# A CIN and tower kernel on one core: the tower run in two groups of batch rows, the context share summed in PSUM, and five ACT banks for each tile of the last chunk

## The chip, the cores and the metric

The kernel runs on one core of a Trainium2 chip. The metric is the device time of one execution, in microseconds (us). Before the change it is 917.98 us, the median of 3 runs (917.52 to 918.87).

## The reference, cut to what matters

For each of 512 batch rows, 32 embedding rows of 32 numbers are gathered (`e`). Two layers of outer products follow, then a small tower of three dense layers.

```python
z = einsum('bhd,bmd->bhmd', e, prev)         # prev = e in layer 0, cur in layer 1
cur = relu(einsum('bpd,pn->bnd', z, W[0]))   # n = 128; layer 1 has 32 * 128 products p
z = sum(concatenate([cur0, cur1], axis=1), axis=-1)   # pooled over d: 256 numbers a row
h = concatenate([z, dense_ctx], axis=1)      # 256 + 16 = 272 numbers a row
h = maximum(h @ W_top1 + b_top1, 0.0)        # 512
h = maximum(h @ W_top2 + b_top2, 0.0)        # 256
y = h @ W_top3                               # 1
```

## The kernel before

**Tiles and banks.** The 512 rows are four blocks of 128 (`BT = 4`). A chunk is one block and four values of d (`DC = 4`), so there are 32 chunks and 128 tiles (`TILES`), a tile being 128 rows and one d. Layer 1 of a tile is 8 banks of 128x512: a bank is four fields h of 128 outputs each, made by three passes of TensorE (`three_passes`: high by high, high by low, low by high, all 512 columns). What TensorE writes for a field must still be scaled by the embedding number of that row and field, and the 32 fields be added up. The banks of a tile are shared between two engines. The first `DQ` of them (4, 3, 4, 3 for the four tiles of a chunk) go through the PSUM tile `yd` (3 buffers) to VectorE, which scales and adds in one instruction a field (`add_bank`). The other 4 or 5 (`AQ`) go through `ya` (2 buffers) to ScalarE, which only scales them into `scaled` (`scale_bank`).

**What is done with ScalarE's part.** GpSimd starts a DMA that adds one half of the tile's first four banks to the other (`halve`), then adds what is left (`sum_up`: L310, L314 only for a fifth bank, L318) into `part`. VectorE starts its chains from `part`, so that it waits for it in its first bank. At a tile's end `join_chains` adds the two chains, and `add_to_sum1` adds the tile into the pooled sum of its block, `pooled1_b`.

**Order.** Every engine runs an order written out by hand, each instruction with the semaphores that it waits for. TensorE goes through slots, one for each tile: in a slot it makes in turn an A bank (for ScalarE) of this tile and a D bank (for VectorE) of the tile three before (`LAG = 3`). After the slot of tile 127 there are no A banks, and D banks of tiles 125, 126 and 127 alone are left. While a chunk runs, layer 0 of the next one is made between its slots.

**The tower** comes after the last tile, for all 512 rows at once. TensorE transposes the pooled sums (L742), ScalarE copies them to SBUF (L495), and TensorE multiplies four pieces of `W_top1` by `pooled0` (L746) and by `pooled1` (L749). VectorE adds `ctx_share` (L642), which is the context's part of layer 1 with the bias, computed at the start of the program (L655 on TensorE, L394 on ScalarE). ScalarE applies the relu (L498), TensorE makes layer 2 (L754), ScalarE its bias and relu (L501), TensorE layer 3 (L760), ScalarE the copy of y (L504), and a DMA from SP's queue writes it. All matmuls of the tower have plain float32 operands; a matmul of them has two records in the trace. Those of the banks have one for each pass.

## Time and profile before

| | |
|---|---|
| device time, median of 3 runs | 917.98 us |
| the profiled execution's own time | 913.96 us |
| its span in the trace | 911.6 us |
| busy TensorE (PE) | 837.5 us, 92% |
| busy VectorE (DVE) | 763.2 us, 84% |
| busy ScalarE (ACT) | 764.8 us, 84% |
| busy GpSimd (POOL) | 661.3 us, 73% |

The span runs from the first to the last instruction or transfer. The profiled execution took 2.36 us more than its span, and 4.02 us less than the median of the three unprofiled runs. Busy time of PE is that of its matmul records, which overlap where they are pipelined, so the start of one to the start of the next is the better measure of what a matmul costs. PEld is TensorE's load of the stationary operand.

### The profile page before, as it was taken

The numbers are of one execution on the slowest core, as the hardware profiler recorded it, in microseconds if no ns is written. First come the engines' busy times: TensorE is split into PE (matmuls) and PEld (weight loads), VectorE is DVE, ScalarE is ACT, GpSimd is POOL, SyncE is SP. The second block draws the span as 40 slices with busy tenths as digits, with TensorE's granted clock in tenths as the row PEclk, the third lists the DMA queues.
The fourth block names the chain that finished last, engine by engine and source line by source line (L and its number), as shares of the span: only waits on it lengthen the run. The fifth ranks groups of instructions, "written<-read, shape, count | busy, mean of one in ns | idle before, by whom it ended". The sixth has DMA issues, their size and how long they took to land.

```text
span 911.6 us, 14382 instructions
## 1 busy us (share of the span) xinstructions
PE 837.5 (92%) x3572; PEld 670.4 (74%) x3572; DVE 763.2 (84%) x2400; ACT 764.8 (84%) x2568; POOL 661.3 (73%) x630
## 2 busy tenths in 40 slices
PE   0317999999999999999999999999999999999988
PEld 0114788887888888887888888878888888888753
DVE  0214799998999999998999999988999999999891
ACT  0315999999999999999999999999999999999842
POOL 6773788887878888887888788865776666667550
PEclk9999999999999999999999999999999999999998
DMA  9145767667766667677676776677666776764430
GB/s 269 17 108 159 164 152 163 145 159 182 165 155 164 144 154 166 154 156 171 158 163 156 159 167 155 145 161 170 152 153 152 165 162 151 157 155 91 84 70 0
DMA packets 57717, 133.83 MB, mean 147 GB/s; under 512 B 8785, under 2 KB 22321, under 8 KB 57538
## 3 DMA queue, kind: packets, MB, share of 16 engines
q0 software_dynamic: 22528, 69.22, 42.1%
q1 hardware_dynamic: 32178, 59.94, 20.2%
q10 hardware_dynamic: 2928, 3.76, 1.4%
q8 instruction: 28, 0.46, 0.2%
q14 instruction: 55, 0.45, 0.1%
HBM read 62.64 MB, written 5.24 MB: 74 GB/s over the span
## 4 chain that ended last, share of the span: by engine, by line
PE 85%; ACT 5%; POOL 4%; DVE 2%; issue 2%; DMA 2%; SPq 0%; DVEq 0%
PE ya L659 14%; PE ya L660 14%; PE ya L661 14%; PE yd L659 10%; PE yd L661 10%; PE yd L660 10%; POOL emb L287 4%; ACT scaled L444 3%; PE acc L659 3%; PE acc L661 3%; PE acc L660 3%; DVE acc L579 1%; DMA x<-xt_scratch 1%; PE acc L682 1%; PE ya L754 1%
## 5 line engine op out<-in xcount | busy, mean ns | idle before, releaser
L444 ACT ACTIVATE scaled<-ya,emb 128x128 f32<-128x128 f32 x2304 | 661.9, 386 | 56.0 <-PE ya L661 49.7
L579 DVE SCALAR_TENSOR_TENSOR acc<-yd,emb,acc 128x128 f32<-128x128 f32 x1408 | 397.0, 341 | 8.1 <-PE yd L661 7.5
L310 POOL TENSOR_TENSOR quarter<-scaled 128x512 f32<-128x512 f32 x128 | 195.8, 1530 | 62.2 <-DMA scaled<-scaled 46.2
L659 PE MATMUL ya<-w_hi,prev_hi 128*128 128x512 f32 x576 | 227.7, 395 | 6.5 <-ACT scaled L444 4.8
L660 PE MATMUL ya<-w_lo,prev_hi 128*128 128x512 f32 x576 | 225.3, 391 | 0.0
L661 PE MATMUL ya<-w_hi,prev_lo 128*128 128x512 f32 x576 | 225.1, 391 | 0.0
L303 POOL DMA_DIRECT2D scaled<-scaled x128 | 117.8, 920 | 104.7 <-ACT scaled L444 94.3
L659 PE MATMUL yd<-w_hi,prev_hi 128*128 128x512 f32 x448 | 175.2, 391 | 2.1 <-DVE pooled_b L598 1.8
L661 PE MATMUL yd<-w_hi,prev_lo 128*128 128x512 f32 x448 | 174.4, 389 | 0.0
L660 PE MATMUL yd<-w_lo,prev_hi 128*128 128x512 f32 x448 | 174.3, 389 | 0.0
L287 POOL DMA_INDIRECT emb<-in_tbl,idx x128 | 134.6, 1052 | 30.7 <-issue 27.2
L659 PEld LDWEIGHTS ya<-w_hi,prev_hi 128*128 128x128 f32 x576 | 108.6, 189 | 36.0 <-ACT scaled L444 11.2
L661 PEld LDWEIGHTS ya<-w_hi,prev_lo 128*128 128x128 f32 x576 | 108.7, 189 | 23.1
L660 PEld LDWEIGHTS ya<-w_lo,prev_hi 128*128 128x128 f32 x576 | 108.8, 189 | 21.5
L531 DVE TENSOR_TENSOR prod<-xb,xm_ps 128x512 f32<-128x512 f32 x128 | 87.7, 685 | 31.1 <-DMA xb<-xt_scratch 27.6
L579 DVE SCALAR_TENSOR_TENSOR acc<-yd,emb,part 128x128 f32<-128x128 f32 x256 | 77.7, 345 | 37.3 <-PE yd L661 32.5
L318 POOL TENSOR_TENSOR part<-quarter 128x256 f32<-128x256 f32 x128 | 100.4, 784 | 10.0
L659 PEld LDWEIGHTS yd<-w_hi,prev_hi 128*128 128x128 f32 x448 | 84.1, 188 | 22.8 <-DVE pooled_b L598 2.9
L661 PEld LDWEIGHTS yd<-w_hi,prev_lo 128*128 128x128 f32 x448 | 84.1, 188 | 17.6
L660 PEld LDWEIGHTS yd<-w_lo,prev_hi 128*128 128x128 f32 x448 | 84.1, 188 | 17.4
L536 DVE TENSOR_TENSOR lo<-prod,hi 128x512 fp32r<-128x512 f32 x128 | 87.2, 681 | 11.5 <-ACT hi L424 11.5
L314 POOL TENSOR_TENSOR quarter<-quarter,scaled 128x512 f32<-128x512 f32 x64 | 82.8, 1294 | 5.0
(69 smaller groups left out, 711.2 us busy)
## 6 DMA issues: line engine op xcount, KB each, us to landing
scaled<-scaled POOLq DMA_DIRECT2D x128, 512.0 KB, 6.7
xb<-xt_scratch SPq DMA_DIRECT2D x64, 512.0 KB, 5.4
x<-xt_scratch SPq DMA_DIRECT2D x64, 192.0 KB
xm<-xt_scratch SPq DMA_DIRECT2D x32, 256.0 KB, 3.0
emb<-in_tbl,idx POOLq DMA_INDIRECT x128, 3.9
scaled<-in_L_rec_filter SPq DMA_DIRECT2D x8, 256.0 KB, 6.3
xt_scratch<-xt_stage SPq DMA_DIRECT2D x7, 256.0 KB, 3.3
xt_scratch<-xt_stage SPq DMA_DIRECT2D x9, 128.0 KB, 3.3
```

The source lines that it names most:

```text
L287: pool.indirect_dma_start(emb[:, bt, D * f:D * (f + 1)], None, tables[f], bass.IndirectOffsetOnAxis(ap=idx[:, bt, f:f + 1], axis=0)).then_ ...
L303: pool.dma_start(piece[:, 0:2 * C], piece[:, 2 * C:4 * C], accum_op=ALU.add).then_inc(halved[tile % PR], 16)
L310: pool.tensor_tensor(four, piece[:, 0:C], piece[:, C:2 * C], ALU.add).then_inc(quartered, 1)
L314: pool.tensor_tensor(four, four, piece[:, 4 * C:5 * C], ALU.add).then_inc(quartered, 1)
L318: pool.tensor_tensor(part[:, tile % PR].rearrange("p i n -> p (i n)"), four[:, 0:2 * N], four[:, 2 * N:4 * N], ALU.add).then_inc(part_read ...
L444: op = act.activation(scaled[:, tile % PR, C * j + N * i:C * j + N * (i + 1)], ya[:, n % RA, N * i:N * (i + 1)], ACT.Copy, scale=scale_of( ...
L531: dve.tensor_tensor(prod[:], xb[:, k, :], xm_ps[:], ALU.mult).then_inc(product_ready, 1)
L536: dve.tensor_tensor(lo[:, n % 2, :], prod[:], hi[:, n % 2, :].bitcast(F32), ALU.subtract).then_inc(lo_ready, 1)
L579: dve.scalar_tensor_tensor(after, y_part, scale_of(tile, HB * j + i), before, ALU.mult, ALU.add).then_inc(chained, 1)
L659: pe.matmul(dst, v_hi, m_hi, start=start, stop=False)
L660: pe.matmul(dst, v_hi, m_lo, start=False, stop=False)
L661: return pe.matmul(dst, v_lo, m_hi, start=False, stop=stop)
```

## The change

**Banks.** In the last chunk every tile has 3 D banks and 5 A banks (`DQ_LAST`), where tiles 124 and 126 had 4 and 4. The functions `dq(tile)` and `aq(tile)` take the place of the tuples.

**The last tile's part.** GpSimd adds the five A banks of tile 127 one by one (`sum_last`), with no DMA. VectorE doesn't start that tile's chains from `part`: its first two instructions only scale, and two more add the two halves of `part` after the join.

**The tower** is done in two groups of rows: `EARLY_B`, the 384 rows of the first three blocks, and `LAST_B`, the 128 of the last. The context's part is a matmul that starts the accumulation of layer 1 (`tower_ctx`), so that L655, L394, L498 and L642 of before are gone, and the bias goes into ScalarE's relu (`relu_h1`). TensorE's part for the early rows stands between the slots of the last tiles, and the PSUM tiles are others.

The diff, cut to its core (lines of the changed program; long definitions of semaphores and lines in which only `dq` and `aq` take the place of a tuple are left out):

```diff
@@ -36,8 +36,9 @@
     TILES = DC * CHUNKS
     HB = C // N
     DQ = (4, 3, 4, 3)
-    AQ = tuple(F // HB - n for n in DQ)
-    A_CHUNK, D_CHUNK = sum(AQ), sum(DQ)
+    DQ_LAST = (3, 3, 3, 3)
+    A_CHUNK, D_CHUNK = DC * F // HB - sum(DQ), sum(DQ)
+    A_MOST = F // HB - min(DQ)
...
-        tower_ps = [yd[:, 0, :], yd[:, 1, :], yd[:, 2, :], prod[:]]
+        tower_ps = [prod[:], xm_ps[:], ya[:, 0, :], ya[:, 1, :]]
         h1 = scaled[:, 0, 0:4 * C].rearrange("p (q c) -> p q c", q=4)
-        h1_sum = scaled[:, 1, 0:4 * C].rearrange("p (q c) -> p q c", q=4)
         h2 = xb[:, 0:H2 // P, :]
         y = small[0:1, :]
+        EARLY_B, LAST_B = slice(0, B - P), slice(B - P, B)
...
         def d_number(tile, j):
 
-            return D_CHUNK * (tile // DC) + sum(DQ[:tile % DC]) + j
+            return sum(dq(t) for t in range(tile)) + j
+
+        last_banks = [yd[:, d_number(TILES - 1, j) % RD, :] for j in range(RD)]
...
-            return HB * d_number(tile, 0) + tile
+
+            return HB * d_number(tile, 0) + tile + 2 * (tile == TILES)
...
 
+            def sum_last():
+
+                tile = TILES - 1
+                piece, four = scaled[:, tile % PR, :], quarter[:, tile % 2, :]
+                pool.wait_ge(part_ready, tile - 1)
+                for j in range(1, aq(tile)):
+                    pool.wait_ge(a_used, a_number(tile // DC, tile % DC, j) + 1)
+                    before = piece[:, 0:C] if j == 1 else four
+                    if j > 1:
+                        pool.wait_ge(last_added, j - 1)
+                    pool.tensor_tensor(four, before, piece[:, C * j:C * (j + 1)], ALU.add).then_inc(last_added, 1)
+                    if j == 2:
+                        sum_up(tile - 1)
+                pool.wait_ge(last_added, aq(tile) - 1)
+                pool.tensor_tensor(part[:, tile % PR].rearrange("p i n -> p (i n)"), four[:, 0:2 * N], four[:, 2 * N:4 * N],
+                                   ALU.add).then_inc(part_ready, 1)
+
...
                 for q in range(DC):
+                    if DC * c + q == TILES - 1:
+                        sum_last()
+                        continue
                     halve(DC * c + q)
...
-            def copy_ctx_share(q):
-                act.wait_ge(ctx_mm, q + 1)
-                act.activation(ctx_share[:, q, :], yd[:, q % 2, :], ACT.Identity,
-                               bias=bt1_sb[:, q:q + 1]).then_inc(ctx_share_ready, 1)
-
             act.wait_ge(tower_loaded, 16 * 6)
-            for q in range(H1 // P):
-                copy_ctx_share(q)
 
...
-            act.wait_ge(pooled1_turned, 1)
-            act.activation(pooled1[:], acc0[:].rearrange("p (t b) -> p t b", t=BT), ACT.Copy).then_inc(pooled1_ready, 1)
-            for q in range(H1 // P):
-                act.wait_ge(tower_sum, q + 1)
-                act.activation(h1[:, q, :], h1_sum[:, q, :], ACT.Relu).then_inc(tower_relu, 1)
-            act.wait_ge(tower_mm, H1 // P + H2 // P)
-            for q in range(H2 // P):
-                act.activation(h2[:, q, :], ya[:, q, :], ACT.Relu,
-                               bias=bt2_sb[:, q:q + 1]).then_inc(tower_relu, 1)
-            act.wait_ge(tower_mm, H1 // P + H2 // P + 1)
-            act.activation(y, acc0[0:1, :], ACT.Copy).then_inc(y_ready, 1)
...
+            copy_pooled1(0, slice(0, BT - 1))
+            act.wait_ge(part_ready, TILES - DC + 1)
+            relu_h1(0, EARLY_B)
+            relu_h2(0, 0, EARLY_B, acc0[:])
+            copy_pooled1(1, slice(BT - 1, BT))
+            relu_h1(1, LAST_B)
+            relu_h2(1, 0, EARLY_B, last_banks[0])
+            relu_h2(0, 1, LAST_B, last_banks[2])
+            relu_h2(1, 1, LAST_B, acc0[:])
+            copy_y(0, EARLY_B, last_banks[0])
+            copy_y(1, LAST_B, prod[:])
...
                 if j == 0:
-                    dve.wait_ge(part_ready, tile + 1)
+                    if tile < TILES - 1:
+                        dve.wait_ge(part_ready, tile + 1)
...
-                    dve.scalar_tensor_tensor(after, y_part, scale_of(tile, HB * j + i), before,
-                                             ALU.mult, ALU.add).then_inc(chained, 1)
+                    if tile == TILES - 1 and j == 0 and i < 2:
+                        dve.tensor_scalar(after, y_part, scale_of(tile, i), None, ALU.mult).then_inc(chained, 1)
+                    else:
+                        dve.scalar_tensor_tensor(after, y_part, scale_of(tile, HB * j + i), before,
+                                                 ALU.mult, ALU.add).then_inc(chained, 1)
...
+                base = chain_base(tile) + HB * dq(tile)
+                dve.wait_ge(chained, base)
                 dve.tensor_tensor(total, total, acc[:, tile % 2, 0, :], ALU.add).then_inc(chained, 1)
+                if tile == TILES - 1:
+                    dve.wait_ge(part_ready, TILES)
+                    for i in range(2):
+                        dve.wait_ge(chained, base + 1 + i)
+                        dve.tensor_tensor(total, total, part[:, tile % PR, i, :], ALU.add).then_inc(chained, 1)
...
-            dve.wait_ge(ctx_share_ready, H1 // P)
-            for q in range(H1 // P):
-                dve.wait_ge(tower_mm, q + 1)
-                dve.tensor_tensor(h1_sum[:, q, :], tower_ps[q], ctx_share[:, q, :], ALU.add).then_inc(tower_sum, 1)
...
-            pe.wait_ge(tower_loaded, 16 * 6)
-            for q in range(H1 // P):
-                if q > 1:
-                    pe.wait_ge(ctx_share_ready, q - 1)
-                pe.matmul(yd[:, q % 2, :], wt1_ctx[:, P * q:P * (q + 1)], ctx_t[:], start=True,
-                          stop=True).then_inc(ctx_mm, 1)
...
+            def tower_ctx(q, rows):
+                pe.matmul(tower_ps[q][:, rows], wt1_ctx[:, P * q:P * (q + 1)], ctx_t[:, rows], start=True, stop=False)
+
+            def tower_pooled0(q, rows):
+                pe.matmul(tower_ps[q][:, rows], wt1_sb[:, 0, P * q:P * (q + 1)],
+                          pooled0[:, rows.start // P:rows.stop // P], start=False, stop=False)
+
+            def tower_pooled1(q, rows, bts):
+                pe.matmul(tower_ps[q][:, rows], wt1_sb[:, 1, P * q:P * (q + 1)], pooled1[:, bts],
+                          start=False, stop=True).then_inc(l1_mm, 1)
...
-            pe.wait_ge(ctx_share_ready, H1 // P)
+            pe.wait_ge(tower_loaded, 16 * 6)
...
-            pe.wait_ge(summed1, TILES)
-            for t in range(BT):
-                turn = pe.transpose(acc0[:, P * t:P * (t + 1)], pooled1_b[:, t, :], identity[:])
-            turn.then_inc(pooled1_turned, 1)
+                    if DC * c + q == TILES - 2:
+                        tower_ctx(0, EARLY_B)
+                        tower_ctx(1, EARLY_B)
+                    if DC * c + q == TILES - 1:
+                        pe.wait_ge(folded0, 2 * (BT - 1))
+                        tower_pooled0(0, EARLY_B)
+                        tower_pooled0(1, EARLY_B)
+                    if DC * c + q == TILES:
+                        pe.wait_ge(a_used, a_number(CHUNKS - 1, DC - 1, aq(TILES - 1) - 1) + 1)
+                        pe.wait_ge(summed1, DC * CPB * (BT - 1))
+                        for t in range(BT - 1):
+                            turn = pe.transpose(acc0[:, P * t:P * (t + 1)], pooled1_b[:, t, :], identity[:])
+                        turn.then_inc(pooled1_turned, 1)
+                        tower_ctx(2, EARLY_B)
+                        tower_pooled0(2, EARLY_B)
+                    if DC * c + q == TILES + 1:
+                        tower_ctx(3, EARLY_B)
+                        tower_pooled0(3, EARLY_B)
+                        pe.wait_ge(pooled1_ready, 1)
+                        for q1 in range(H1 // P):
+                            tower_pooled1(q1, EARLY_B, slice(0, BT - 1))
+
+            def layer2(m, n, rows, bank):
+
+                for t in range(H1 // P):
+                    pe.wait_ge(h1_ready, n * H1 // P + t + 1)
+                    mm = pe.matmul(bank[:, 0:rows.stop - rows.start], wt2_sb[:, t, P * m:P * (m + 1)], h1[:, t, rows],
+                                   start=t == 0, stop=t == H1 // P - 1)
+                mm.then_inc(l2_mm, 1)
+
+            def layer3(n, rows, bank):
+                pe.wait_ge(h2_ready, (n + 1) * H2 // P)
+                for m in range(H2 // P):
+                    mm = pe.matmul(bank[0:1, 0:rows.stop - rows.start], wt3_sb[:, m:m + 1], h2[:, m, rows],
+                                   start=m == 0, stop=m == H2 // P - 1)
+                mm.then_inc(l3_mm, 1)
+
+            layer2(0, 0, EARLY_B, acc0[:])
             pe.wait_ge(folded0, 2 * BT)
             for q in range(H1 // P):
-                pe.matmul(tower_ps[q], wt1_sb[:, 0, P * q:P * (q + 1)], pooled0[:], start=True, stop=False)
-            pe.wait_ge(pooled1_ready, 1)
+                tower_ctx(q, LAST_B)
+                tower_pooled0(q, LAST_B)
+            pe.wait_ge(summed1, TILES)
+            pe.transpose(last_banks[1][:, 0:P], pooled1_b[:, BT - 1, :], identity[:]).then_inc(pooled1_turned, 1)
+            pe.wait_ge(pooled1_ready, 2)
             for q in range(H1 // P):
-                pe.matmul(tower_ps[q], wt1_sb[:, 1, P * q:P * (q + 1)], pooled1[:],
-                          start=False, stop=True).then_inc(tower_mm, 1)
-            for t in range(H1 // P):
-                pe.wait_ge(tower_relu, t + 1)
-                for q in range(H2 // P):
-                    mm = pe.matmul(ya[:, q, :], wt2_sb[:, t, P * q:P * (q + 1)], h1[:, t, :],
-                                   start=t == 0, stop=t == H1 // P - 1)
-                    if t == H1 // P - 1:
-                        mm.then_inc(tower_mm, 1)
-            for t in range(H2 // P):
-                pe.wait_ge(tower_relu, H1 // P + t + 1)
-                mm = pe.matmul(acc0[0:1, :], wt3_sb[:, t:t + 1], h2[:, t, :], start=t == 0, stop=t == H2 // P - 1)
-            mm.then_inc(tower_mm, 1)
+                tower_pooled1(q, LAST_B, slice(BT - 1, BT))
+            layer2(1, 0, EARLY_B, last_banks[0])
+            layer2(0, 1, LAST_B, last_banks[2])
+            layer2(1, 1, LAST_B, acc0[:])
+            layer3(0, EARLY_B, last_banks[0])
+            layer3(1, LAST_B, prod[:])
 
```

**TensorE, end of the program, before.** The rows begin with the last D bank of tile 127. L742 transposes the four blocks of `pooled1_b`, L746 and L749 are layer 1 (`yd` and `prod` hold it) and L754 is layer 2 of the tower.

```order
L659 MATMUL yd<-w1_hi,prev_hi 128x512 [waits summed1]
L660 MATMUL yd<-w1_lo,prev_hi 128x512
L661 MATMUL yd<-w1_hi,prev_lo 128x512
L742 MATMUL acc0<-identity,pooled1_b 128x128 [waits summed1]
L742 MATMUL acc0<-identity,pooled1_b 128x128 x3
L746 MATMUL yd<-pooled0,wt1_sb 128x512 [waits folded0]
L746 MATMUL yd<-pooled0,wt1_sb 128x512 x2
L746 MATMUL prod<-pooled0,wt1_sb 128x512
L749 MATMUL yd<-pooled1,wt1_sb 128x512 [waits pooled1_ready]
L749 MATMUL yd<-pooled1,wt1_sb 128x512 x2
L749 MATMUL prod<-pooled1,wt1_sb 128x512
L754 MATMUL ya<-scaled,wt2_sb 128x512 [waits tower_relu]
```

**TensorE, the changed program, from the last D bank of tile 126 (L700 to L702) to the first pass of tile 127.** L731 is `tower_ctx`, L734 `tower_pooled0`, L738 `tower_pooled1`, each on 384 rows.

```order
L700 MATMUL yd<-w1_hi,prev_hi 128x512 [waits summed1]
L701 MATMUL yd<-w1_lo,prev_hi 128x512
L702 MATMUL yd<-w1_hi,prev_lo 128x512
L731 MATMUL ya<-ctx_t,wt1_ctx 128x384
L734 MATMUL ya<-pooled0,wt1_sb 128x384
L738 MATMUL prod<-pooled1,wt1_sb 128x384 [waits pooled1_ready]
L738 MATMUL xm_ps<-pooled1,wt1_sb 128x384
L738 MATMUL ya<-pooled1,wt1_sb 128x384 x2
L700 MATMUL yd<-w1_hi,prev_hi 128x512 [waits chained]
L701 MATMUL yd<-w1_lo,prev_hi 128x512
L702 MATMUL yd<-w1_hi,prev_lo 128x512
L700 MATMUL yd<-w1_hi,prev_hi 128x512 [waits chained]
```

Six matmuls of the tower have come to stand between the two tiles. Two `tower_ctx` stand in the same way ahead of the slot of tile 127, two `tower_pooled0` ahead of the D banks of tile 125, and three transposes, one `tower_ctx` and one `tower_pooled0` behind them.

**TensorE, the changed program, from the last pass of tile 127.** L817 is layer 2 of the tower (on `scaled`, which holds h1), L834 the transpose of the last block.

```order
L702 MATMUL yd<-w1_hi,prev_lo 128x512
L817 MATMUL acc0<-scaled,wt2_sb 128x384 [waits h1_ready] x4
L731 MATMUL prod<-ctx_t,wt1_ctx 128x128 [waits folded0]
L734 MATMUL prod<-pooled0,wt1_sb 128x128
L731 MATMUL xm_ps<-ctx_t,wt1_ctx 128x128
L734 MATMUL xm_ps<-pooled0,wt1_sb 128x128
L731 MATMUL ya<-ctx_t,wt1_ctx 128x128
L734 MATMUL ya<-pooled0,wt1_sb 128x128
L731 MATMUL ya<-ctx_t,wt1_ctx 128x128
L734 MATMUL ya<-pooled0,wt1_sb 128x128
L834 MATMUL yd<-identity,pooled1_b 128x128 [waits summed1]
L738 MATMUL prod<-pooled1,wt1_sb 128x128 [waits pooled1_ready]
```

Layer 2's first half for the early rows, and the context and layer-0 shares of the last rows, have come to stand between the last bank and the transpose, which waits for the last tile as L742 did. Behind these rows follow the other three `tower_pooled1` (128 columns), layer 2 with 4 matmuls of 384 and 8 of 128 columns, and layer 3 with 2 and 2.

**GpSimd, from the DMA for tile 126 on, before.** L303 is `halve`; the last three rows are `sum_up` of tile 127, which waits for its DMA (`halved_3`).

```order
L303 DMA scaled<-scaled 128x1024 [waits a_used]
L310 TENSOR_TENSOR quarter<-scaled 128x512 [waits halved_2,part_ready]
L318 TENSOR_TENSOR part<-quarter 128x256 [waits chained,quartered]
L310 TENSOR_TENSOR quarter<-scaled 128x512 [waits halved_3,part_ready]
L314 TENSOR_TENSOR quarter<-quarter,scaled 128x512 [waits a_used,quartered]
L318 TENSOR_TENSOR part<-quarter 128x256 [waits chained,quartered]
```

**GpSimd, from `sum_up` of tile 125 on, after.** L342 and L346 are `sum_last`.

```order
L329 TENSOR_TENSOR part<-quarter 128x256 [waits chained,quartered]
L342 TENSOR_TENSOR quarter<-scaled 128x512 [waits a_used,part_ready]
L342 TENSOR_TENSOR quarter<-quarter,scaled 128x512 [waits last_added,a_used]
L321 TENSOR_TENSOR quarter<-scaled 128x512 [waits halved_2,part_ready]
L325 TENSOR_TENSOR quarter<-quarter,scaled 128x512 [waits a_used,quartered]
L329 TENSOR_TENSOR part<-quarter 128x256 [waits chained,quartered]
L342 TENSOR_TENSOR quarter<-quarter,scaled 128x512 [waits last_added,a_used] x2
L346 TENSOR_TENSOR part<-quarter 128x256 [waits last_added]
```

The DMA for tile 127 is gone, and the sum of tile 126 stands between the second and the third of the additions of tile 127.

## Rows read from the trace of the kernel before

**Rows 1.** The page's first part: busy us (share) xinstructions.
```profile
span 911.6 us, 14382 instructions
PE 837.5 (92%) x3572; PEld 670.4 (74%) x3572; DVE 763.2 (84%) x2400; ACT 764.8 (84%) x2568; POOL 661.3 (73%) x630
```

**Rows 2.** Busy time by stretch (start:end, length, busy by engine), last 51.6 us.
```profile
core 0: us, PE busy (x) PEld busy (x) DVE busy (x) ACT busy (x) POOL busy (x), PEclk, DMA share, GB/s
860.00:875.60 15.60, 15.60 (x69) 12.34 (x68) 12.70 (x46) 13.91 (x50) 12.22 (x13) 1.00 0.53 101
875.60:889.50 13.90, 9.07 (x31) 4.81 (x29) 13.43 (x51) 1.14 (x4) 6.22 (x6) 0.95 0.21 39
...
892.00:894.00 2.00, 2.00 (x4) 0.77 (x3) 0.00 (x0) 0.00 (x0) 0.00 (x0) 0.50 0.00 0
...
896.00:898.00 2.00, 2.00 (x6) 0.85 (x5) 0.68 (x1) 0.00 (x0) 0.00 (x0) 1.00 0.00 0
```

**Rows 3.** The chain that ended last, its end: start, us, what.
```profile
889.23 0.30 DVE pooled_b L598
...
890.70 4.80 PE yd L746 x6
895.49 0.86 PE prod L746 x2
896.35 2.58 PE yd L749 x6
...
899.78 6.88 PE ya L754 x16
...
906.69 0.70 ACT xb L501
...
907.43 1.89 PE acc L760 x4
...
909.35 0.59 ACT small L504
```

**Rows 4.** Timeline of the last chunk (start, us, engine line), PE, ACT and DVE.
```profile
864.37 0.50 PE L659 MATMUL ya<-w_hi,prev_hi 128*128 128x512 f32 x1
864.53 3.37 ACT L444 ACTIVATE scaled<-ya,emb 128x128 f32<-128x128 f32 x12 [0.22 <-PE ya L661]
...
865.17 0.40 PE L659 MATMUL yd<-w_hi,prev_hi 128*128 128x512 f32 x1
865.86 0.40 PE L659 MATMUL ya<-w_hi,prev_hi 128*128 128x512 f32 x1
...
875.59 0.39 PE L659 MATMUL yd<-w_hi,prev_hi 128*128 128x512 f32 x1
...
885.67 0.60 DVE L579 SCALAR_TENSOR_TENSOR acc<-yd,emb,part 128x128 f32<-128x128 f32 x2
...
889.58 1.12 PE L742 MATMUL acc<-identity,pooled_b 128*128 128x128 f32 x4 [2.80 <-DVE pooled_b L598]
```

**Rows 5.** Timeline at 211 us, where block 1 is transposed.
```profile
210.96 0.57 PEld L668 LDWEIGHTS ya<-identity,emb_sorted 128*128 128x128 f32 x4
211.17 0.60 PE L668 MATMUL ya<-identity,emb_sorted 128*128 128x128 f32 x4
```

**Rows 6.** Groups by form, last 32 us and 20 to 48 us: busy, mean ns, idle before.
```profile
L754 PEld LDWEIGHTS ya<-scaled,wt_sb 128*128 128x128 f32 x16 | 3.0, 190 | 3.8 <-issue 3.8
...
L402 ACT ACTIVATE emb_sorted<-emb 128x256 f32<-128x256 f32 x1 | 0.4, 416 | 9.1 <-DMA emb<-in_tbl,idx 9.1
```

**Rows 7.** Timeline of GpSimd for tile 127.
```profile
876.69 0.87 POOL L303 DMA_DIRECT2D scaled<-scaled  x1 [1.38 <-issue]
...
881.78 1.28 POOL L310 TENSOR_TENSOR quarter<-scaled 128x512 f32<-128x512 f32 x1 [2.09 <-DMA scaled<-scaled]
883.14 1.28 POOL L314 TENSOR_TENSOR quarter<-quarter,scaled 128x512 f32<-128x512 f32 x1
884.50 0.73 POOL L318 TENSOR_TENSOR part<-quarter 128x256 f32<-128x256 f32 x1
```

70 lines of the change are left out of this document (44 added, 26 removed).

## The prediction

> **What bounds the kernel now.** I read the page's busy times first: PE 92% of the span, DVE and ACT 84% [rows 1]. That is an average over two different programs, so I read stretches next. Up to 875.6 us PE has no idle time and the granted clock is 1.00 [rows 2]: the banks bound it. A bank is three passes, 0.69 us (an A bank starts at 865.86 where the D bank before it started at 865.17 [rows 4]); one that has waited takes 0.80 (864.37 to 865.17). From 875.6 to 889.5 PE is busy 9.07 us of 13.90 and VectorE 13.43: VectorE bounds the last ten D banks. From 889.5 on nothing is left but the tower, and the chain of waits shows it as one line: PE, ACT, PE, ACT [rows 3]. From the transposes at 889.58 to the end of the span at 911.6 are 22.0 us. The reader should see two prices there for one kind of record. `L746` takes 4.80 us for 6 records, `L749` 2.58 for 6: 0.43 us a record of 512 columns, and about 0.85 at the start, where the granted clock is 0.50, that is 1.2 in place of 2.4 GHz, after TensorE had waited 2.8 us for VectorE [rows 2 to 4]. The six records cost 2.2 us more than `L749`'s six, and the four transposes 0.5 more than four at full clock (1.12 [rows 4] and 0.60 [rows 5]).
>
> **The start of the program.** The removed `L655` and `L394` lie ahead of 47 us, where ScalarE then sits idle 9.1 us for a gathered embedding [rows 6]. They were hidden; I take nothing for them. If that cover were gone it would be the gathers that are slower, which nothing here touches.
>
> **Prices.** A plain float32 record costs 0.43 us for 512 columns at full clock [rows 3], so 0.32 for 384, and a matmul is two records. For 128 columns there is no such matmul in the trace. By its share it would be 0.107 a record. The nearest row is the transposes at full clock: four records of 128x128 in 0.60 us with the last one's drain, 0.15 each at the very most [rows 5]. A load of weights shows 0.19 us [rows 6]; were that the pitch, a record would cost 0.19, and 0.30 if load (0.19) and matmul (0.107) came one after the other. I take 0.125, nearest to the transposes. ScalarE's 128-column instruction has a pitch of 3.37/12 = 0.28 and a wait of 0.22 for TensorE's drain [rows 4]; a lone one I put at 0.35, between that and the 0.70 of a 512-column one with bias [rows 3].
>
> **Leg 1, up to the first D bank of tile 125 on TensorE (before: 875.59 [rows 4]).** I carried the starts forward bank by bank over the last chunk. (a) 33 banks come before it where there were 32: 0.69. (b) Two `tower_ctx` and two `tower_pooled0` of 384 columns for the same groups stand ahead of it: 8 records, 2.58. (c) Two more A banks for ScalarE. It needs 1.12 us for one and TensorE 0.69, so that two A banks in a row cost little (the wait ahead of 864.37 is some 0.04 and 0.11 of restart) but a third in a row, as now from tile 124 to 125, costs 1.12 - 0.69 = 0.43 and a restart. With five such neighbours instead of three, and the place ahead of tile 127 covered by `tower_ctx`, I get 0.8. Sum 4.1: the bank starts at 879.7. All of this was free time for VectorE and is now on the path, because in leg 2 TensorE sets the end.
>
> **Leg 2, from there to the last transpose.** Before: 875.59 to 889.58, 14.0 us, by VectorE. Now TensorE has 9 D banks (6.2), three transposes (0.4), `tower_ctx` and `tower_pooled0` for two groups (8 records, 2.6), four `tower_pooled1` (8 records, 2.6), layer 2's first half (8 records, 2.6) and 16 records of 128 columns (2.0): 16.3 us, with no wait among them. VectorE does it sooner. The first bank of tile 127 starts 6 banks (4.1), 0.4, 2.6 and 2.6 after the leg's start, so at 9.7; VectorE follows 0.9 later, and needs 3.9 for a tile of three banks (885.67 to 889.52 [rows 3, 4]) and 0.7 for the two extra additions: 15.2. So the end of the tiles, at about 894.9, comes 5.4 us later than before, and the transpose at 896.0 even later, 1.1 us after it could. Leg 2 grows by 2.3.
>
> GpSimd is not late. For tile 127 the first addition began 4.2 us behind `L303`'s end, then it took 1.28 + 1.28 + 0.73 [rows 7]. The sum of tile 126, now between the additions of tile 127, ends by my carrying forward at about 884, and VectorE wants it at 884.8. If it came up to 2 us late, VectorE's idle time ahead of tile 127 would take it. The last `part` is ready near 887.5 and wanted at 893.8.
>
> **Leg 3, from the transpose to the end.** Before 22.0. Now: transpose, drain, ScalarE's copy of 128 columns and the handovers 0.8; then on TensorE 8 records of `tower_pooled1` (1.0), 8 of layer 2 on 384 columns (2.6), 16 on 128 (2.0), layer 3 with 4 of 384 (1.3) and 4 of 128 (0.5), 7.4 in sum; ScalarE's relus fall beside it, since each group is followed by another group's matmuls. Then drain and ScalarE's copy of y, 0.6, and from its end to the span's 1.66 as before (909.94 to 911.6 [rows 3]). Sum 10.5, so 11.5 less. Three things are in it: the work that has moved into legs 1 and 2, VectorE's step `L642` taken out of the handovers, and the full clock, since TensorE has no long idle stretch before it any more. Of the clock row 0.50 [rows 2] stands only behind the wait of 2.8 us, and plain float32 matmuls alone brought it back to 1.00 at 896.
>
> **Sum.** +4.1 +2.3 -11.5 = -5.1 to -5.2 us. Against the profiled execution: 913.96 - 5.2 = 908.8 (span 906.4). The median of the unprofiled runs lies 4.02 above the profiled one, so 912.8.
>
> **A rule against it.** The rows bound a small record by 0.107 and 0.30, with the transposes' 0.15 between. The Trainium skill, page "TensorE: Matmul & The Clock Gate", section "Back-to-back issue gap", says that in a stream of weight loads and matmuls both set the spacing, and gives about 81 ns for a matmul of 128 columns. At two passes a record that is an estimate of 0.16 by this page, and for 44 small records 1.6 us more: 914.4. No run here has shown it; the transposes (0.15 at most) leave room for it.
>
> **Rivals.**
> (1) The load of weights sets the pitch of small records: between the 0.15 of [rows 5] and 0.19 [rows 6]. There are 44 of them (16 in leg 2, 28 in leg 3), so 1.1 to 2.9 more: 913.9 to 915.7. For it speaks that `PEld` fills 0.57 of the four transposes' 0.60 [rows 5]; against, that four of 0.19 would fill 0.76. Chance 0.13. The Trainium skill's estimate above lies in this rival's middle.
> (2) Load and matmul don't overlap at 128 columns: 0.30 a record, 44 x 0.175 = 7.7 more: 920.5, slower. It decides from 0.125 + (5.2 + 1.84)/44 = 0.285 a record on. Against it: the four transposes would have taken 1.2 us and took 0.60. Chance 0.03.
> (3) The clock is at 0.50 from the last transpose on, as it was. TensorE's 7.4 us double: 920.2, slower. If it is there for the first 5 us as before, some 2.5 more: 915.3. Against: TensorE's only wait in leg 3 is some 0.7 us, where it was 2.8 before the transposes. Chance 0.03 for the whole, 0.05 for the part.
> (4) The early tower costs what it saves: TensorE's handovers to ScalarE in leg 3 (five where TensorE could wait, 0.22 of drain, 0.35 and a handover each) are not covered, and the A banks cost another 1.5 us. Together 4 to 5 us: 917.5, no change. Against: every wait has another group's matmuls ahead of it. Chance 0.06.
> (5) Small records at 0.107 and no loss by A banks: 1.6 less, 911.2. Chance 0.10.
>
> **How the numbers follow.** The forecast has 0.60, (5) 0.10, (1) 0.13, the part of (3) 0.05, (4) 0.06, (2) and (3) 0.06. The runs before spread by 1.35 us, so a difference under 0.2%, 1.84 us, is about what a measurement can't tell from no change. Faster is below 916.1: the forecast, (5), most of (1) and of the part of (3), 0.86. Within 0.2%: (4) and a rest, 0.08. Slower: 0.06. The range takes in (5) and (1): 910.8 to 916.3.
>
> **What would show it.** Right: the first D bank of tile 125 near 879.7; no idle time on PE from there to the transpose near 896; granted clock 1.00 throughout; VectorE idle some 2 us ahead of tile 127; small records near 0.125 apart; 10.5 us from the last transpose to the end. Wrong: small records over 0.19 apart; a row of the clock at 0.50 behind 890; VectorE's last addition behind PE's last small matmul; PE waiting for ScalarE in layer 2.

## The result and the profile after

The changed kernel takes 915.66 us (median of 21 runs, 913.46 to 922.0); the kernel before, on the same chip, 918.45 (21 runs, 915.07 to 920.37). The ratio is 0.9978, with a 95% interval of 0.9968 to 0.9988: faster by 2.0 us by the ratio, 2.8 by the medians, where 5.2 had been forecast. The direction was right; the size is 0.4 of the forecast's by the ratio and a little over half by the medians. The median itself, 915.66, lies inside the forecast's range (910.8 to 916.3) and where rival (1) had put it (913.9 to 915.7); that is luck, since rival (1)'s cause isn't what the runs show.

**A measure of the end.** The profiled execution of the changed kernel is its slowest: 922.0 us, span 920.0, and it comes to the last chunk 10.0 us later than that of before (863.28 against 853.26, below), which belongs to this execution and not to the change: in e1, e2 and e3 below, changed kernels too, it is reached at 852.8 to 854.1. So the ends are compared from a fixed point, GpSimd's start of the DMA for tile 123, to the end of the span. This is the row of it (start, us, engine and line, what was waited for) in GpSimd's timeline of the changed kernel:

```profile
863.28 0.87 POOL L314 DMA_DIRECT2D scaled<-scaled  x1 [1.31 <-ACT scaled L467]
```

The changed kernel has 920.0 - 863.28 = 56.7 us from there; the kernel before, where the same row stands at 853.26, 911.6 - 853.26 = 58.3. The expectations of the first four experiments count from the first A bank of tile 124, which starts 0.1 to 0.2 us sooner (56.9 and 58.5). By this measure the execution shown gained 1.6 us. The end of a kernel is read from one execution each.

**The page.** Its first part, which answers to [rows 1]: 44 more records on PE, and less busy time.

```profile
span 920.0 us, 14478 instructions
PE 836.3 (91%) x3616; PEld 676.0 (73%) x3616; DVE 762.0 (83%) x2390; ACT 764.9 (83%) x2580; POOL 663.8 (72%) x633
```

**Stretches.** The windows of the changed kernel's end, as in [rows 2] (start:end, length, busy PE, PEld, DVE, ACT, POOL, granted clock, DMA share, GB/s):

```profile
889.80:908.40 18.60, 18.60 (x72) 11.92 (x71) 11.97 (x44) 3.85 (x8) 6.12 (x6) 1.00 0.01 2
905.20:908.60 3.40, 3.40 (x18) 2.42 (x17) 0.68 (x3) 0.58 (x1) 0.00 (x0) 1.00 0.00 0
909.30:911.00 1.70, 1.70 (x9) 1.70 (x10) 0.00 (x0) 1.00 (x3) 0.00 (x0) 0.50 0.00 0
911.00:912.70 1.70, 1.70 (x4) 0.92 (x4) 0.00 (x0) 0.46 (x2) 0.00 (x0) 0.54 0.00 0
912.70:915.00 2.30, 2.30 (x13) 1.64 (x12) 0.00 (x0) 0.48 (x1) 0.00 (x0) 1.00 0.00 0
```

PE is not idle from 889.8 to the last transpose at 908.44, as was forecast. Behind it TensorE waits 0.37 us for ScalarE's copy, and then the clock is at 0.50 for 3.4 us. In [rows 2] that stood behind an idle time of 2.8 us. Three rows of PE's timeline: the first D bank of tile 125, the last transpose, and the matmul behind it with its wait.

```profile
889.72 0.68 PE L700 MATMUL yd<-w_hi,prev_hi 128*128 128x512 f32 x1
908.44 0.27 PE L834 MATMUL yd<-identity,pooled_b 128*128 128x128 f32 x1
909.08 0.76 PE L738 MATMUL prod<-pooled,wt_sb 128*128 128x128 f32 x2 [0.37 <-ACT pooled L520]
```

**The chain that ended last**, of the changed kernel, from the two `tower_ctx` ahead of tile 127 on (start, us, what); it answers to [rows 3]:

```profile
881.60 0.84 PE prod L731 x2
882.44 0.65 PE xm_ps L731 x2
...
892.26 0.33 PE acc L802 x3
892.59 0.84 PE ya L731 x2
893.43 0.84 PE ya L734 x2
...
896.36 0.84 PE ya L731 x2
897.19 0.84 PE ya L734 x2
898.04 0.65 PE prod L738 x2
...
902.70 2.58 PE acc L817 x8
905.27 0.41 PE prod L731 x2
905.69 0.42 PE prod L734 x2
...
908.60 0.12 PE yd L834
...
909.08 0.76 PE prod L738 x2
...
911.12 4.25 PE yd L817 x16
915.37 0.89 PE acc L817 x8
916.26 1.40 PE yd L824 x4
```

One matmul (two records) of 384 columns takes 0.65 us as `L738`, and 0.84 as `L731` or `L734` where these two take turns. The two `L731` at 881.60 stand one behind the other: the first, behind a bank, takes 0.84, and the second 0.65. At 128 columns it is 0.41 where they take turns; the 8 records of `L817` at 915.37 take 0.89, so 0.22 a matmul. `L731` is `tower_ctx`, whose weights (the stationary operand) have 16 rows, one for each number of the context: the timeline of the changed kernel prints 16 partitions for them and 128 for their neighbour (operands and output, partitions x elements).

```profile
905.21 0.48 PE L731 MATMUL prod<-ctx_t,wt_ctx 16*128 16x128 f32 x2
905.62 0.49 PE L734 MATMUL prod<-pooled,wt_sb 128*128 128x128 f32 x2
906.04 0.48 PE L731 MATMUL xm_ps<-ctx_t,wt_ctx 16*128 16x128 f32 x2
```

### The profile page after: what moved, and what is told of

It is laid out like the page before. It is cut to its first block, busy times and chain, and to the rows that moved or that the text cites. A ratio compares the mean times of both kernels' runs of the same rounds, so it can differ in the third digit from the quotient of the medians.

```text
span 920.0 us, 14478 instructions
## 1 busy us (share of the span) xinstructions
PE 836.3 (91%) x3616; PEld 676.0 (73%) x3616; DVE 762.0 (83%) x2390; ACT 764.9 (83%) x2580; POOL 663.8 (72%) x633
## 4 chain that ended last, share of the span: by engine, by line
PE 84%; issue 6%; ACT 5%; DMA 2%; SPq 2%; another core or an unknown queue 1%; DVE 0%; DVEq 0%; ACTq 0%
PE ya L700 14%; PE ya L702 13%; PE ya L701 13%; PE yd L702 10%; PE yd L700 10%; PE yd L701 10%; ACT scaled L467 3%; PE acc L700 3%; PE acc L701 3%; PE acc L702 3%; DMA x<-xt_scratch 2%; SPq L240 1%; PE acc L723 1%; ACT hi L447 1%
## 5 line engine op out<-in xcount | busy, mean ns | idle before, releaser
L700 PE MATMUL ya<-w_hi,prev_hi 128*128 128x512 f32 x578 | 229.6, 397 | 15.2 <-ACT scaled L467 8.9
L702 PE MATMUL ya<-w_hi,prev_lo 128*128 128x512 f32 x578 | 226.1, 391 | 0.0
L700 PE MATMUL yd<-w_hi,prev_hi 128*128 128x512 f32 x446 | 174.5, 391 | 0.0
L702 PE MATMUL yd<-w_hi,prev_lo 128*128 128x512 f32 x446 | 173.7, 390 | 0.0
L700 PEld LDWEIGHTS ya<-w_hi,prev_hi 128*128 128x128 f32 x578 | 109.2, 189 | 46.9 <-ACT scaled L467 17.7
L702 PEld LDWEIGHTS ya<-w_hi,prev_lo 128*128 128x128 f32 x578 | 109.3, 189 | 23.2
L329 POOL TENSOR_TENSOR part<-quarter 128x256 f32<-128x256 f32 x127 | 97.5, 767 | 10.0
L700 PEld LDWEIGHTS yd<-w_hi,prev_hi 128*128 128x128 f32 x446 | 83.7, 188 | 17.9
L702 PEld LDWEIGHTS yd<-w_hi,prev_lo 128*128 128x128 f32 x446 | 83.7, 188 | 17.5
L447 ACT ACTIVATE hi<-prod 128x512 fp32r<-128x512 f32 x128 | 78.9, 616 | 13.0 <-DVE prod L574 7.1
```

The costliest lines, as they stand in the source:

```text
L329: pool.tensor_tensor(part[:, tile % PR].rearrange("p i n -> p (i n)"), four[:, 0:2 * N], four[:, 2 * N:4 * N], ALU.add).then_inc(part_read ...
L447: act.activation(hi[:, n % 2, :], prod[:], ACT.Copy).then_inc(hi_ready, 1)
L700: pe.matmul(dst, v_hi, m_hi, start=start, stop=False)
L702: return pe.matmul(dst, v_lo, m_hi, start=False, stop=stop)
```

## The experiments

Two theories stood at first. **Switches:** a matmul behind one with another number of weight rows (16 behind 128, or 128 behind 16) costs some 0.2 us more, and the fall of the clock has to do with the 16-row matmuls. **Small records:** matmuls of 128 columns are dear in themselves (rival (1)), and the clock falls by the short wait for ScalarE (rival (3)).

All ratios are to the kernel before on the same chip, 913.5 us (17 runs) for the first four, 913.86 (29) for the next four, 913.44 (15) for the last two. Diffs are cut to their core, with `...` for what is left out.

"End" is the measure above. "Full clock" counts the executions whose mean granted clock was 1.000 to three digits; with one stretch of 3.4 us at half clock it reads 0.998, with two 0.996. The mean doesn't say where in the program a stretch lay. The profiled execution of the changed kernel (0.996) had one behind 909.1 and one between 110 and 120 us; that of the kernel before (0.996) had 6.8 us in one piece, from 888 on. The changed kernel had 9 of 21 at full clock (median 914.71), nine at 0.998 (916.74) and three at 0.996. The kernel before had 3 of 61 at full clock, 35 at 0.998 and 23 lower, so its end of 58.3 is one with the longer fall. Of the seven kernels below that hold the clock in the end, 47 of 48 executions read 1.000, so a stretch elsewhere in the program is rare.

| run | what it is | ratio | end, us | full clock |
|---|---|---|---|---|
| changed | the change whole | 0.9978 | 56.7 | 9 of 21 |
| e1 | changed, last rows' matmuls grouped | 0.9950 | 53.9 | 5 of 6 |
| e2 | changed, context padded to 128 rows | 0.9937 | 52.4 | 5 of 5 |
| e3 | changed, banks put back | 0.9981 | 54.2 | 4 of 12 |
| e4 | changed, context's share kept | 0.9915 | 50.7 | 5 of 5 |
| e5 | before, with the banks alone | 1.0015 | 59.4 | 0 of 12 |
| e6 | before, with the context alone | 1.0012 | 59.6 | 0 of 12 |
| e7 | e4, fillers moved | 0.9904 | 49.3 | 5 of 5 |
| e8 | before, idle time filled | 0.9976 | 55.5 | 12 of 12 |
| e9 | e6, padded | 0.9982 | 55.6 | 11 of 11 |
| e10 | e7, banks put back | 0.9901 | 48.3 | 4 of 4 |

**e1, the last rows' matmuls grouped.** The eight matmuls of 128 columns no longer take turns: first four of the context, then four of `pooled0`.

```diff
             for q in range(H1 // P):
                 tower_ctx(q, LAST_B)
+            for q in range(H1 // P):
                 tower_pooled0(q, LAST_B)
```

> The changed kernel with one reordering: for the last 128 rows, the four context matmuls come first and then the four pooled0 matmuls, where they alternated. From the trace of the changed kernel the end of the program (first A bank of tile 124 to the end of the span) is 56.9 us, against 58.5 before. Theory A (each switch between a matmul with 16 rows of weights and one with 128 costs some 0.2 us, because the load isn't pulled ahead): the eight matmuls take 2.2 us in place of 3.3, so 55.8. If the slow records are also what lets the granted clock fall to 0.50 at 909 us, it doesn't fall here, and 1.7 us more go: 54.1. Rival (128-column records cost 0.2 in that place whatever stands beside them): 3.3 us as in the changed kernel, 56.9.

909.83 us, ratio 0.995 (0.9937 to 0.9963), end 53.9, full clock in 5 of 6. The timeline of PE in e1:

```profile
895.95 0.48 PE L731 MATMUL prod<-ctx_t,wt_ctx 16*128 16x128 f32 x2
896.28 0.38 PE L731 MATMUL xm_ps<-ctx_t,wt_ctx 16*128 16x128 f32 x2
896.50 0.60 PE L731 MATMUL ya<-ctx_t,wt_ctx 16*128 16x128 f32 x4
897.03 0.49 PE L734 MATMUL prod<-pooled,wt_sb 128*128 128x128 f32 x2
...
898.03 0.27 PE L835 MATMUL yd<-identity,pooled_b 128*128 128x128 f32 x1
```

From the first of them to the transpose it is 898.03 - 895.95 = 2.1 us, where it was 908.44 - 905.21 = 3.2. The same eight matmuls in another order: so the price is that of the switch, not of 128 columns. And the clock stays up, which gives the other 1.7 us. Both were expected (54.1).

**e2, the context padded to 128 rows.** The order is that of the changed kernel; `ctx_t` and `wt1_ctx` get 128 partitions, the added ones zero, and the sums are the same.

```diff
-        ctx_t = sb("ctx_t", [D_CTX, B])
+        ctx_t = sb("ctx_t", [P, B])
...
-        wt1_ctx = sb("wt1_ctx", [D_CTX, H1])
+        wt1_ctx = sb("wt1_ctx", [P, H1])
...
+            dve.memset(ctx_t[:], 0.0).then_inc(padded, 1)
+            dve.memset(wt1_ctx[:], 0.0).then_inc(padded, 1)
```

> The changed kernel with the context's two operands padded with zeros from 16 to 128 partitions; the order stays alternating, the sums are the same. Theory A (the switch between 16 and 128 rows costs): all eight matmuls of the last rows run at 0.11 us a record, 1.8 us in place of 3.3, and each context matmul of 384 columns behind a pooled0 one or ahead of one at 0.65 in place of 0.84: about 1.0 more; the end of the program takes 54.4 us, or 52.7 if the clock then doesn't fall. Rival (alternating weights between two tensors, or short matmuls as such, cost it): no change, 56.9.

907.83 us, ratio 0.9937 (0.9924 to 0.995), end 52.4, full clock in 5 of 5. The timeline of PE in e2, where the two kinds take turns again:

```profile
893.45 0.39 PE L735 MATMUL prod<-ctx_t,wt_ctx 128*128 128x128 f32 x2
893.67 0.39 PE L738 MATMUL prod<-pooled,wt_sb 128*128 128x128 f32 x2
...
895.24 0.27 PE L838 MATMUL yd<-identity,pooled_b 128*128 128x128 f32 x1
```

0.22 us a matmul, 1.8 for the eight. Taking turns is harmless if the rows are equal in number. Behind the transpose TensorE waits 0.37 us for ScalarE in e1 and e2 as in the changed kernel, and the clock stays at 1.00 in both, so this wait alone doesn't let it fall. e2 ends 1.5 us sooner than e1, and in e1 eight matmuls still stand behind one with another number of rows: five of 384 columns (0.84 in place of 0.65 in the chain), the first pass of the bank behind `tower_ctx` ahead of tile 127 (0.43 in place of 0.23), and the first of each group of 128 columns (0.41 in place of 0.22). 8 x 0.19 = 1.5. The changed kernel has fourteen such places: 14 x 0.19 = 2.7, and 56.7 - 1.7 - 52.4 = 2.6 is what e2 saves beside the clock.

**e3, the banks put back.** The tower as changed, the last chunk's banks as before.

```diff
-    DQ_LAST = (3, 3, 3, 3)
+    DQ_LAST = (4, 3, 4, 3)
```

> The changed kernel with the banks of the last chunk as before (4, 3, 4, 3 for VectorE). Theory (TensorE sets the end, so that a bank moved from VectorE to ScalarE gives nothing and costs the wait for three A banks in a row): the loss by A banks goes (some 0.8 us in the last chunk), the tenth D bank comes behind the A banks (+0.7): the end of the program within 0.5 us of 56.9. Rival (VectorE would set the end without the five ACT banks): the end of the tiles comes up to 1.0 us later than in the changed kernel for each of two banks, 57.9 to 58.9.

911.22 us, ratio 0.9981 (0.997 to 0.9991), end 54.2 in an execution at full clock; full clock in 4 of 12. By the times nothing is lost without the fifth A banks (0.9981 beside 0.9978). The changed kernel at full clock would have an end of 56.7 - 1.7 = 55.0, so by the ends, one execution each, e3 is 0.8 shorter, where at most 0.5 had been expected. The times don't show this gain. The clock falls about as often as with the change whole.

**e4, the context's share kept.** The share is computed at the start, as before, and VectorE adds it in place, for the early rows behind tile 126 and for the last at the end. TensorE has no `tower_ctx`.

```diff
+            def add_share(n, rows):
+                for q in range(H1 // P):
+                    dve.wait_ge(l1_mm, n * H1 // P + q + 1)
+                    dve.tensor_tensor(ctx_share[:, q, rows], tower_ps[q][:, rows], ctx_share[:, q, rows],
+                                      ALU.add).then_inc(tower_sum, 1)
...
             for q in range(H1 // P):
-                tower_ctx(q, LAST_B)
                 tower_pooled0(q, LAST_B)
```

> The changed kernel, but the context's share is computed at the start of the program as before and added by VectorE (384 columns between tiles 126 and 127, 128 columns after tile 127), so that TensorE makes no context matmul at the end. Theory (TensorE is the bound of the end, and the context matmuls with their switches cost it about 6 us: 1.5 ahead of tile 127, 2.1 for two of 384 columns with the switch of pooled0 behind them, 2.5 for the last rows): TensorE loses its place as bound to VectorE in the stretch of D banks, the end of the program gets 4 to 6 us shorter: 51 to 53 us, and the time 910 to 912 us. Rival (VectorE's step in the handovers costs what TensorE saves): 56 to 57 us.

906.72 us, ratio 0.9915 (0.9901 to 0.9928), end 50.7, full clock in 5 of 5. That is a little below the 51 to 53 expected. The context on TensorE cost the change 6.0 us of 56.7. Of these 1.7 are the clock and 2.6 the switches; the last 1.7 (52.4 - 50.7) is what even equal rows cost. The context's matmuls themselves are 4 x 0.65 + 4 x 0.22 = 3.5 us; the rest of that doesn't come back, since VectorE now sets the end. Its added work shows in its timeline in e4 ahead of tile 127, and in PE's at the last transpose:

```profile
889.99 1.01 DVE L664 TENSOR_TENSOR ctx_share<-ya,ctx_share 128x384 f32<-128x384 f32 x2
890.91 0.60 DVE L631 TENSOR_SCALAR acc<-yd,emb 128x128 f32<-128x128 f32 x2
```
```profile
895.55 0.33 PE L849 MATMUL yd<-identity,pooled_b 128*128 128x128 f32 x1 [0.42 <-DVE pooled_b L658]
```

Now TensorE waits 0.42 us for VectorE: the two are nearly even, with VectorE the later.

**e5, the banks alone,** on the kernel before: `DQ_LAST = (3, 3, 3, 3)` and `sum_last`, with the tower untouched.

```diff
-    AQ = tuple(F // HB - n for n in DQ)
-    A_CHUNK, D_CHUNK = sum(AQ), sum(DQ)
+    DQ_LAST = (3, 3, 3, 3)
+    A_CHUNK, D_CHUNK = DC * F // HB - sum(DQ), sum(DQ)
...
```

> The kernel before with the banks' part alone: five ACT banks a tile in the last chunk and the last tile's part added at the end; the tower as before. The measure is from GpSimd's DMA issue for tile 123 to the end of the span: 58.3 us before. Theory (the five ACT banks are worth nothing by themselves: the first D bank of tile 125 comes 1.5 us later, VectorE has one bank less behind it, 1.0, and two additions more, 0.7): 58.3 to 59.5, the time the same or up to 0.1% slower. Rival (VectorE bounds the end, so that two banks fewer are 1 to 2 us): 56.5 to 57.3.

915.38 us, ratio 1.0015 (1.0003 to 1.0026), end 59.4, full clock in 0 of 12. Slower by 1.4 us (1.1 by the end); the end is within the 58.3 to 59.5 expected. The chain of e5 shows where it waits:

```profile
882.72 0.74 POOL part L329
883.53 0.93 DVE acc L613 x4
...
891.28 0.31 DVE yd L629
891.61 0.30 DVE pooled_b L638
```

The chain runs through GpSimd's sum of tile 126, which `sum_last` puts between the additions of tile 127, and then through VectorE, which ends at 891.91 where it ended at 889.53 [rows 3], although the fixed points are only 0.6 us apart. This run has both the fifth banks and `sum_last`, and doesn't tell what each of them costs.

**e6, the context alone,** on the kernel before: four `tower_ctx` of 512 columns behind the last D bank, in the time in which TensorE waited 2.8 us; the bias goes into ScalarE's relu, and VectorE's `L642` is gone.

```diff
+            for q in range(H1 // P):
+                pe.matmul(tower_ps[q], wt1_ctx[:, P * q:P * (q + 1)], ctx_t[:], start=True, stop=False)
             pe.wait_ge(summed1, TILES)
...
```

> The kernel before with the context's part alone: four context matmuls of 512 columns stand behind the last D bank, ahead of the wait for the last tile, and accumulate with the rest; ScalarE's relu takes the bias, VectorE's addition is gone. One group of rows, banks as before. TensorE was idle there for 2.8 us and they take 3.5. Theory (the idle stretch is what let the granted clock fall, and filling it keeps it at 1.00): 2.7 us from the clock and 0.8 from VectorE's step, 0.7 lost: 55.5 us by the measure of 58.3 before. Rival (the clock falls anyway, since the D banks leave TensorE half idle for 12 us): 58.3.

915.07 us, ratio 1.0012 (1.0002 to 1.0023), end 59.6, full clock in 0 of 12. TensorE doesn't wait for the last tile any more, VectorE's step is gone from the chain, and yet the kernel is slower, against the expectation (55.5) and its rival (58.3) both. The windows of e6 (columns as above):

```profile
887.20:889.00 1.80, 1.80 (x5) 0.81 (x5) 1.80 (x9) 0.00 (x0) 0.00 (x0) 0.97 0.00 0
889.00:892.40 3.40, 3.40 (x5) 1.00 (x3) 0.91 (x4) 0.00 (x0) 0.00 (x0) 0.50 0.00 0
892.40:895.80 3.40, 3.40 (x8) 1.92 (x8) 0.00 (x0) 0.60 (x1) 0.00 (x0) 0.51 0.00 0
```

PE is busy throughout, with 16-row matmuls from 887.2 on, and the clock falls at 888.9, in this execution for 6.8 us (five of the twelve read 0.998, one stretch of 3.4). So filling the wait isn't enough to hold it. Ahead of 887.2 TensorE still waits between the last D banks (1.02 and 0.73 us at the longest), as in the kernel before; e9 below has such waits too.

**e7, the fillers moved.** e4, with `tower_pooled0` of the early rows taken out of the last chunk's banks and put behind the tiles 125 and 126, and two of the four matmuls of layer 2's second half for the early rows put ahead of the wait for ScalarE's copy.

```diff
-                    if DC * c + q == TILES - 1:
-                        pe.wait_ge(folded0, 2 * (BT - 1))
-                        tower_pooled0(0, EARLY_B)
-                        tower_pooled0(1, EARLY_B)
...
+            layer2(1, 0, EARLY_B, last_banks[0], range(0, 2))
             pe.wait_ge(pooled1_ready, 2)
...
-            layer2(1, 0, EARLY_B, last_banks[0])
+            layer2(1, 0, EARLY_B, last_banks[0], range(2, 4))
```

> The kernel with the kept context share (50.65 us by that measure) and the tower's early matmuls moved: no pooled0 matmul ahead of tile 125's D banks, two with the transposes behind them, two behind tile 126's; and half of layer 2's matmuls for the early rows stand in the wait for the last copy of pooled sums. Theory (in that kernel VectorE waits 1.7 us for tile 125 because of the two pooled0 matmuls, and TensorE 0.6 us for the copy): 1.3 + 0.6 us less, 48.8. Rival (the D banks of tile 126 or 127 come late in their place): 50 to 51.

905.16 us, ratio 0.9904 (0.9886 to 0.9922), end 49.3, full clock in 5 of 5: 9.0 us less than before by the end. It was expected at 48.8, with 50 to 51 as the rival. In the chain of e7 the wait for ScalarE's copy has 1.29 us of matmuls over it:

```profile
893.12 0.30 DVE pooled_b L658
...
893.47 0.33 PE yd L849
893.80 1.29 PE yd L832 x4
895.09 0.22 PE prod L759 x2
```

**e8, the idle time filled.** The kernel before, with three matmuls of 128 rows and 512 columns in TensorE's wait; nothing reads them, and the output is the same.

```diff
+            for q in range(3):
+                pe.matmul(xm_ps[:], wt1_sb[:, 0, P * q:P * (q + 1)], wt1_sb[:, 0, :], start=True, stop=True)
             pe.wait_ge(summed1, TILES)
```

> The kernel before with three matmuls of 512 columns whose result nothing reads, behind the last D bank, where TensorE was idle 2.8 us; they take 2.6. It measures the clock by itself. Theory: the granted clock stays at 1.00, the ten records that ran at half of it take 2.7 us less: 55.6 us by the measure, where before is 58.3. Rival (the fall comes from the half idle stretch ahead, not from this wait): 58.3 and a row of the clock at 0.50.

911.98 us, ratio 0.9976 (0.9966 to 0.9987), end 55.5, full clock in 12 of 12. The timeline of PE in e8:

```profile
887.37 2.74 PE L741 MATMUL xm_ps<-wt_sb 128*128 128x512 f32 x6
890.34 0.66 PE L744 MATMUL acc<-identity,pooled_b 128*128 128x128 f32 x4 [0.23 <-DVE pooled_b L598]
890.83 2.74 PE L748 MATMUL yd<-pooled,wt_sb 128*128 128x512 f32 x6
```

The six records that took 4.80 us [rows 3] take 2.6, as `L749`'s did. Three unread matmuls bring 2.8 us by the end and 2.2 by the ratio: as much as the whole change. The end gives more, since it is compared with an execution with the longer fall (6.8 us), and more than half of those of the kernel before have the shorter one.

**e9, e6 padded.** The context's matmuls of e6 with zeros up to 128 rows, as in e2.

```diff
-        ctx_t = sb("ctx_t", [D_CTX, B])
+        ctx_t = sb("ctx_t", [P, B])
...
-        wt1_ctx = sb("wt1_ctx", [D_CTX, H1])
+        wt1_ctx = sb("wt1_ctx", [P, H1])
...
```

> The kernel with the context's part alone (59.6 us by the measure), with the context's operands padded with zeros to 128 partitions; nothing else differs, and the matmuls have the same columns. There the granted clock fell to 0.50 although TensorE had no idle time ahead of the transposes, since 16-row matmuls filled it. Theory (matmuls of 16 rows don't hold the clock, matmuls of 128 do, as the unread ones did): the clock stays at 1.00 in all executions, 3.4 us less from it and 0.4 from the two switches, 55.6 to 56.0 us. Rival (what lets the clock fall is the half idle stretch of the D banks, and the unread matmuls helped by being fewer): it falls again, 59 us.

912.1 us, ratio 0.9982 (0.9973 to 0.9991), end 55.6, full clock in 11 of 11. The windows of e9, where e6 stood at 0.50:

```profile
887.30:890.20 2.90, 2.90 (x8) 1.20 (x7) 2.33 (x9) 0.00 (x0) 0.00 (x0) 1.00 0.00 0
890.20:894.00 3.80, 3.80 (x13) 1.96 (x12) 0.00 (x0) 0.60 (x1) 0.00 (x0) 1.00 0.00 0
```

The number of rows alone decides over 4.0 us of the end (59.6 and 55.6), and over 0.3% of the time (1.0012 and 0.9982), some 2.7 us. Of the 4.0, 3.4 are the clock and 0.4 the two switches, ahead of the four matmuls and behind them; the rest is a wait of TensorE for VectorE among the D banks, 1.02 us in e6's execution and 0.73 in e9's. This pair is the cleanest comparison here: the same order, the same columns, nearly the same waits ahead of these matmuls and none among them. Beside e8 (55.5), which leaves VectorE's step in the chain, e9 gains nothing.

**e10, e7 with the banks put back,** by e3's edit.

```diff
-    DQ_LAST = (3, 3, 3, 3)
+    DQ_LAST = (4, 3, 4, 3)
```

> The kernel with the kept share and the moved matmuls (49.3 us by the measure), with the banks of the last chunk as before (4, 3, 4, 3). Theory (VectorE now ends the stretch of D banks, so that a bank moved to ScalarE is worth something at last, but the third A bank in a row costs TensorE as much): within 0.7 us of 49.3. Rival (without TensorE as the bound the five ACT banks give the full 1.0 us of each bank): 50.3 to 51.3.

905.13 us, ratio 0.9901 (0.9886 to 0.9916), end 48.3, full clock in 4 of 4. The same time as e7; by the end 1.0 shorter, where at most 0.7 had been expected, and against the rival, by which the fifth banks would have been worth 1.0 us each.

## Why the prediction was right in direction and wrong in size

**Leg 1 was right, in part by luck.** The first D bank of tile 125 starts at 889.72 in the timeline, 26.4 us behind the fixed point; before it was 875.59 - 853.26 = 22.3. That is +4.1, as predicted. But behind a plain matmul the timeline places a bank's start sooner than the chain does (889.72 and 890.18; where a bank stands before it, as before the change, they are 0.16 apart), and by the chain leg 1 grew by 4.4. Term (b) was too small: the four matmuls take 0.84 + 3 x 0.65 and the bank behind `tower_ctx` 0.2 more, 3.0 for 2.6.

**Leg 2 was mis-sized.** Predicted 16.3 us; from 889.72 to the transpose at 908.44 it is 18.7. The failed step is "Prices": every record was priced by its columns, 0.32 and 0.125, whatever stood beside it. Both prices hold next to a neighbour with as many rows of weights (0.65 / 2 = 0.32, and 0.22 / 2 = 0.11), and neither holds where `tower_ctx` takes turns with `tower_pooled0`. Along the chain, the four matmuls of 384 columns took 4 x 0.84 = 3.4 for 2.6, and the eight of 128 columns 3.3 (905.27 to 908.60) for 2.0: 2.1 of the 2.4 that leg 2 was too long. The other 0.3 is the same 0.3 of the timeline that leg 1 lacks: by the chain leg 2 is 908.60 - 890.18 = 18.4. e1 and e2 show this cause apart from all others. No wait stands in leg 2, as predicted, and VectorE was idle 2.48 us ahead of tile 127, where some 2 had been forecast.

**Leg 3 was mis-sized by the clock.** Predicted 10.5, measured 920.0 - 908.44 = 11.6. At full clock it is 907.9 - 898.03 = 9.9 in e1 and 905.1 - 895.24 = 9.9 in e2, so 0.6 better than predicted (28 small records at 0.11 in place of 0.125 are 0.4 of it), and the 1.7 more are the 3.4 us at half clock. The step that failed is "the full clock, since TensorE has no long idle stretch before it any more". e6, e8 and e9 show what it missed: that TensorE isn't idle was not enough; with 16 rows in its matmuls the clock fell, with 128 it stayed. Rival (3)'s part, with a chance of 0.05, came true in about half of the executions, for 3.4 us where it had put 5.

**The sum, made again.** -5.2 + 2.4 - 0.6 = -3.4 at full clock, for which the nine such executions stand at 914.71 - 918.45 = -3.7. With the clock's 1.7 it is -1.7, and the end of the profiled execution gained 1.6. By the ratio of all executions it is -2.0, and by their medians -2.8, between the two.

**The rivals.** (1) asked for 0.15 to 0.19 a small record, and (5) for 0.107. Measured are 0.11 wherever the rows don't change (e2, e1's groups, and `L817` at 915.37), so (5)'s price was the true one, and the switches and the clock took more than it gave. The rule of the Trainium skill that was weighed (page "TensorE: Matmul & The Clock Gate", section "Back-to-back issue gap") gives 81 ns for a matmul of 128 columns in a stream with weight loads, by which the prediction estimated 0.16 us a record. This case's records don't bear that out: 0.11 a record is 56 ns a pass, if a record is two passes as the prediction took it. (2) asked for 0.30 a record, no overlap of load and matmul in any, and wasn't seen: a switching matmul of 128 columns takes 0.41, which is 0.21 a record, and others 0.11. The 0.19 more comes once a matmul of two records and is as long as one load (0.19 [rows 6]), as if the load alone couldn't start ahead at a switch; that this is the mechanism is only argued. (4) was wrong: TensorE's only wait for ScalarE in leg 3 is 0.37 us, and with the context off TensorE the early tower is worth 58.3 - 50.7 = 7.6 us.

**What the parts are worth.** Of the three, the two groups of rows carry the gain. The context on TensorE took back 6.0 us (e4). The fifth banks bring nothing in the changed kernel (e3) or in e7 (e10), and with `sum_last` they cost 1.4 in the kernel before (e5). e7 and e10, without the context's matmuls, are the best versions: 0.990 of before, some 9 us.

**Left open.** Why the clock falls in some executions of the changed kernel and not in others isn't shown, since all run the same instructions. Once the turns of 16 and 128 rows are grouped, padded or gone, it almost never falls (20 of 21 executions of e1, e2, e4 and e7 are at full clock, 13 of 33 of the changed kernel and e3). What tips it isn't shown, nor whether it is the 16 rows or the time that the switches add: e1 still has all its 16-row matmuls, and 5 of its 6 executions were at full clock. Why a switch costs 0.19 us is open too.

## What to carry to other kernels

Price a matmul by its neighbour as well as by its columns: where the number of rows of weights differs from one to the next, group them or pad the small ones with zeros. Before reshaping a tail for the sake of an idle TensorE, put matmuls with 128 rows whose result nothing reads into the idle time, as e8 does, and see what the clock alone gives back. And work that was hidden at the start (here a share of 16 rows) should not be moved onto the engine that bounds the end, even if it saves a step of another engine.
